# A conditioned attention layer, f32 on one core: four moves in the first two turns of a software pipeline

## The reference

```
xn = ln(x);  q = xn @ Wq + bq;  k = xn @ Wk + bk + (1 - mask) * -1e6;  v = (xn @ Wv + bv) * mask
q = softmax(q, within a head);  k = softmax(k, over the 64 tokens)
att = k^T v per head;           y = q att
scale, shift = split(silu(cond) @ W_emb + b_emb)      # one pair of 256 per batch
out = x + silu(ln2(y) * (1 + scale) + shift) @ W_out + b_out
```

## Time and profile before

| | us |
|---|---|
| median of 3 runs (lowest, highest) | 306.88 (306.3, 309.34) |
| the profiled execution: time | 307.7 |
| its span, first to last instruction | 305.8 |
| TensorE busy | 291.8 (95%) |
| VectorE busy | 272.4 (89%) |
| GpSimd busy | 244.6 (80%) |
| ScalarE busy | 237.0 (77%) |
| TensorE's granted clock, mean | 1.000 of full speed |

### The profile page before, as it was taken

The page is one execution under the profiler, slowest core; times in us unless marked ns, Lnnn a source line. Parts: engine busy times, 40 slices in busy tenths (PEclk is TensorE's granted clock), DMA queues, the critical chain, the costliest instruction groups (busy, mean ns, idle before and its releaser), DMA issues.

```text
span 305.8 us, 14375 instructions
## 1 busy us (share of the span) xinstructions
PE 291.8 (95%) x5528; PEld 248.5 (81%) x5528; DVE 272.4 (89%) x640; ACT 237.0 (77%) x592; POOL 244.6 (80%) x246
## 2 busy tenths in 40 slices
PE   7999789899999999999999999999999999989875
PEld 7578588788989888988889898889888898877655
DVE  5899999989999999999999999999999796967793
ACT  1567758787978988898979888888989798776443
POOL 2275748989998989999998989898999979873470
PEclk9999999999999999999999999999999999999999
DMA  6983430704527080815325180906251341002024
GB/s 198 315 298 109 129 115 5 236 10 117 198 66 248 1 308 1 253 56 176 133 106 203 46 263 1 298 11 231 78 169 71 90 150 53 17 4 72 4 71 137
DMA packets 28445, 38.61 MB, mean 126 GB/s; under 512 B 2433, under 2 KB 20481, under 8 KB 28418
## 3 DMA queue, kind: packets, MB, share of 16 engines
q1 hardware_dynamic: 28000, 37.94, 38.1%
q10 hardware_dynamic: 418, 0.30, 0.3%
HBM read 29.80 MB, written 8.45 MB: 125 GB/s over the span
## 4 chain that ended last, share of the span: by engine, by line
PE 82%; DVE 9%; issue 4%; POOL 2%; DMA 1%; POOLq 1%; ACT 0%; SPq 0%; DVEq 0%
PE bk L1113 27%; PE bv L1113 27%; PE by L1113 15%; PE by L1198 4%; PE by L1177 4%; PE bv L1189 4%; DVE xstat L785 2%; DMA x_all<-in_x 1%; DVE k_t L909 1%; DVE q_s L898 1%; POOLq L45 1%; DVE qmax L890 1%; DVE th L843 1%; POOL xr L485 1%; DVE ystat L986 0%
## 5 line engine op out<-in xcount | busy, mean ns | idle before, releaser
L641 ACT ACTIVATE k_t<-k_t,kmax 128x64 f32<-128x64 f32 x240 | 60.5, 336 | 6.4 <-DVE kmax L916 6.2
L476 POOL TENSOR_TENSOR x_all<-x_all,bo_all 128x1024 f32 (+1 forms) x16 | 40.1, 2508 | 0.2
L436 POOL TENSOR_TENSOR h_lo<-h_s,h_hi 128x512 fp32r<-128x512 f32 x30 | 38.3, 1297 | 0.9 <-ACT h_hi L660 0.8
L445 POOL TENSOR_TENSOR xt_raw<-xt_raw,rows 128x512 f32<-128x512 f32 x28 | 37.0, 1322 | 1.5 <-DMA rows<-rows_dram 1.5
L447 POOL TENSOR_TENSOR xt_raw<-xt_raw,rows 128x512 f32<-128x512 f32 x28 | 36.5, 1303 | 2.2
L286 POOL TENSOR_TENSOR z_s<-z_s,mod_shift 128x512 f32<-128x512 f32 x30 | 30.7, 1044 | 6.8 <-DVE z_s L930 6.8
L595 ACT ACTIVATE y_s<-y_s,yr 128x256 f32<-128x256 f32 x56 | 29.1, 593 | 3.8 <-POOL yr L468 3.8
L1113 PE MATMUL bv<-w_o_hi,h_hi 128*128 128x256 f32 x120 | 31.6, 285 | 0.0
L1113 PE MATMUL bv<-w_o_lo,h_hi 128*128 128x256 f32 x120 | 31.0, 280 | 0.0
L580 ACT ACTIVATE v_s<-bk,small 128x256 f32<-128x256 f32 x32 | 15.1, 474 | 17.7 <-PE bk L1113 16.4
L1113 PEld LDWEIGHTS by<-kv,q_t 32*64 32x64 f32 x2048 | 22.4, 130 | 6.9 <-issue 6.5
(11 more groups left out here) (163 smaller groups left out, 865.9 us busy)
## 6 DMA issues: line engine op xcount, KB each, us to landing
x_all<-in_x SPq DMA_DIRECT2D x15, 512.0 KB, 6.4
out<-x_all SPq DMA_DIRECT2D x15, 512.0 KB, 5.0
xt_raw<-in_x_t SPq DMA_DIRECT2D x14, 512.0 KB, 6.1
rows<-rows_dram SPq DMA_DIRECT2D x14, 512.0 KB, 4.2
off<-in_mask_rows SPq DMA_DIRECT2D x16, 256.0 KB, 6.1
rows_dram<-xr_rows SPq DMA_DIRECT2D x56, 1.0 KB
x_all<-in_x SPq DMA_DIRECT2D x2, 256.0 KB, 3.5
z_s<-in_w_emb SPq DMA_DIRECT2D x1, 512.0 KB, 7.2
```

Source lines behind the costliest of these rows:

```text
L436: nc.gpsimd.tensor_tensor(h_lo[:, c, :], h_s[:, c, :], h_hi[:, c, :].bitcast(fp32), ALU.subtract).then_inc(hlo_d, 1)
L445: nc.gpsimd.tensor_tensor(xc, xc, rows[:, parity, 0, :], ALU.mult).then_inc(xm_d, 1)
L476: nc.gpsimd.tensor_tensor(xg, xg, bo_all[:, :].unsqueeze(1).broadcast_to([P, T, D]), ALU.add).then_inc(xb_d, 1)
L641: last = nc.scalar.activation(kk, kk, ACT.Exp, scale=-1.0, bias=kmax[:, c, n:n + 1])
```

## The change

Four edits, all in turns 0 to 2:

1. W_out. ScalarE makes the high part in turn 0, halving in the same instruction (`weights_o_high`, between the first two `v_tile`). VectorE is left with one fused operation for the low part (`weights_o_low`).
2. The table is written to `bt[1]` (the fourth bank of `by`) in place of `be[1]` (the second). The wait of TensorE for the copies moves from `exp_k_transposed(1)` to the second half of `q_transposed(1)`, and ScalarE's copies from the end of turn 1 to the start of turn 2.
3. Group 1's `xhat`: tiles 2 and 3 go to GpSimd, behind `x_rstd(1)` in turn -1. GpSimd's `x_biased(0)` moves ahead of `x_rstd(2)`, and ScalarE's third `v_tile` of turn 0 ahead of its first exponential. VectorE's order in turn 0 is new: q's maximum and shift come between and ahead of parts of `x_stats(2)`, and `x_rows(2)` moves from ahead of `x_low(1)` to behind `x_stats(3)`.
4. In turn 1 `y_scaled_all(0)` stands ahead of `q_shifted(1, 1, 0)`.

```diff
 (GpSimd, turn -1)
                     x_rstd(1)
+                    pool.wait_ge(xt_d, 2)
+                    pool.wait_ge(xr_d, 8)
+                    for t in (2, 3):
+                        nc.gpsimd.tensor_scalar(xhat[:, t, :], x_all[:, 1, t * D:t * D + D], xr[:, 0, t:t + 1],
+                                                xr[:, 1, t:t + 1], ALU.mult, ALU.add).then_inc(xhat_d, 1)
                     return
...
 (GpSimd, turn 0)
                     k_shifted(0)
                     k_shifted(1)
+                    x_biased(0)
                     x_rstd(2)
...
-                if not last_turn(i):
-                    x_biased(i)
                 if first(i):
                     x_rstd(3)
+                elif not last_turn(i):
+                    x_biased(i)
...
 (ScalarE)
+            def weights_o_high():
+
+                act.wait_ge(wo_in, 16)
+                nc.scalar.activation(w_o_hi[:, :, :], w_o, ACT.Copy, scale=0.5).then_inc(wo_high, 1)
...
             def x_hat_one():
...
-                for t in range(T):
+                for t in (0, 1):
...
             def emb_copied():
...
-                    nc.scalar.activation(emb[:, j, :], be[1][:, j * BATCH:(j + 1) * BATCH], ACT.Identity,
+                    nc.scalar.activation(emb[:, j, :], bt[1][:, j * BATCH:(j + 1) * BATCH], ACT.Identity,
                                          scale=0.5, bias=b_e[:, j:j + 1]).then_inc(emb_out, 1)
...
+                if isinstance(i, int) and i == 2:
+                    emb_copied()
                 if O:
                     y_hat_all(i - 2)
...
                     v_tile(0, 0, 0)
+                    weights_o_high()
                     v_tile(0, 0, 1)
                     x_hat_one()
+                    v_tile(0, 0, 2)
                     k_exp_first(0)
-                    v_tile(0, 0, 2)
                     v_tile(0, 0, 3)
...
                 q_exp(i, par, 0)
-                if second(i):
-                    emb_copied()
...
 (VectorE)
-            def weights_o():
-
-                dve.wait_ge(wo_in, 16)
-                link(nc.vector.tensor_scalar(w_o, w_o, 0.5, None, ALU.mult))
-                split(w_o, w_o_hi, w_o_lo)
+            def weights_o_low():
+
+                dve.wait_ge(wo_high, 1)
+                nc.vector.scalar_tensor_tensor(w_o_lo[:, :, :], w_o, 0.5, w_o_hi[:, :, :].bitcast(fp32),
+                                               ALU.mult, ALU.subtract).then_inc(weights_ready, 1)
...
                 if first(i):
-                    x_stats(2, 0)
-                elif not (isinstance(i, int) and i + 2 >= G):
+                    q_max(0, 0)
+                    q_shifted(0, 0, 0)
+                    x_variances(2, 0, (0, 1, 2))
+                    q_max(0, 1)
+                    q_shifted(0, 0, 1)
+                    x_variances(2, 0, (3,))
+                    x_means(2)
+                    x_low(1, by[:, 2:4, :])
+                    x_stats(3, 1)
+                    x_rows(2)
+                    return
...
                 if second(i):
-                    weights_o()
+                    weights_o_low()
                     silu_cond()
...
-                if B:
-                    y_sums(i - 1)
-                q_shifted(i, par, 0)
-                if B:
+                y_sums(i - 1)
+                if second(i):
+                    y_scaled_all(0)
+                    q_shifted(1, 1, 0)
+                else:
+                    q_shifted(i, par, 0)
                     y_scaled_all(i - 1)
-                    y_stats(i - 1, (0, 1, 2, 3))
+                y_stats(i - 1, (0, 1, 2, 3))
...
 (TensorE)
-                        last = mm(be[1][:, j * BATCH:(j + 1) * BATCH], w_e[c // 2][:, c % 2, j * P:(j + 1) * P],
+                        last = mm(bt[1][:, j * BATCH:(j + 1) * BATCH], w_e[c // 2][:, c % 2, j * P:(j + 1) * P],
...
                 for e in range(2):
-                    if second(g) and e == 1:
-                        pe.wait_ge(emb_out, 2 * C)
                     wait(pe, ys_d, 2 * (g - 1) + 2)
...
                 for c in range(C):
                     wait(pe, ys_d, 2 * g)
+                    if second(g) and c == 1:
+                        pe.wait_ge(emb_out, 2 * C)
```

More of the change, by code:

```diff
@@ L175, in build_layer @@
         wqv_high = sem("wqv_high")
+        wo_high = sem("wo_high")
         mod_ready = sem("mod_ready")
@@ L772, in x_stats, with x_variances @@
             def x_stats(g, parity):
+                x_variances(g, parity, (0, 1, 2, 3))
+                x_means(g)
+            def x_variances(g, parity, tiles):
                 first = isinstance(g, int)
@@ L781, in x_stats @@
                 wait(dve, xr_d, 4 * g)
-                for t in range(T):
+                for t in tiles:
                     if first and g == 0 and t == 2:
@@ L786, in x_stats, with x_means @@
                                        .rearrange("p g n -> p (g n)")).then_inc(xstat_d, 1)
+            def x_means(g):
                 for t in range(T):
@@ L1022, in body @@
                 if first(i):
-                    x_stats(2, 0)
-                elif not (isinstance(i, int) and i + 2 >= G):
+                    q_max(0, 0)
[9 more added lines that the diff above has]
+                    return
+                if not (isinstance(i, int) and i + 2 >= G):
                     x_rows(i + 2)
```

## The result

| | before | changed |
|---|---|---|
| median of 12 runs, us (lowest, highest) | 309.04 (306.3, 311.67) | 305.6 (304.97, 306.77) |
| profiled execution, us (span) | 307.7 (305.8) | 306.03 (304.2) |
| ratio of the compared runs, 95% interval | | 0.9947 (0.9922 to 0.9973) |

The kernel is faster by 0.5% (0.3 to 0.8). The ratio leaves out the most disturbed runs, all of them of the kernel before; that is why the two medians lie 3.4 us apart, more than it says. The profiled pair differs by 1.6 us, where 2.8 were forecast.

The account below looks back on a forecast made before the run. TensorE, busy 291.8 of 305.8 us, bounds the kernel; only its waits in the first two turns can be had. 1.97 + 0.8 + 0.1 = 2.87, rounded to 2.8: 306.88 - 2.8 = 304.1 us, range 302.4 to 306.2.

Parts of the forecast that it names:

- Gap 1: TensorE's wait for y's division, ahead of the table's matmuls in turn 1; forecast to close whole, 1.97 us.
- gap 2: TensorE's wait for ScalarE's copies of the modulation table out of bank 1; forecast to go, 0.8 us.
- VectorE leaves the turn 0.4 us later: Turn 0: q_max(0, 1) and x_rows(2) delay VectorE by 0.4 us; y_product(0) has 1.0 to spare, so no cost.
- just ready: x_rstd(2) on GpSimd ends at 25.9, in time for x_rows(2), moved to about 26.5 on VectorE.
- The slower rival: Chain through GpSimd's x_rstd(2) and VectorE's x_rows(2) delays k's mask and y_product(0); kernel slower above 29.9; chance 0.04.
- point of decision (27.1): Each microsecond x_rstd(2) ends after 27.1 delays k's mask, its exponentials and y_product(0) one for one.
- Late rows: Rival: x_scaled(2) at contended price or late broadcast delays y_hat 1.0 to 1.5 us; gain 1.3 to 1.8; chance 0.17.
- one of those by which the prediction would call itself wrong: Signs of failure: new TensorE wait for y_s L595, xt_hi or xt_lo in turn 2, or idle time in the loop behind.
- VectorE does what it does in the loop: Reason for pricing x_scaled(2) at 5.3 us, the page's mean, from 33 to 38.4.
- Gap 3: TensorE's 0.8 us wait for k's exponential in the first turn; forecast to shrink by 0.1 us.

Follow-up runs that it names:

- e4: Kernel before with only W_out's high part by ScalarE and the division ahead of q's shift; ratio 0.9916.
- e11: Kernel before with only W_out's high part by ScalarE and the fused low part on VectorE; ratio 0.9874.
- e9: Changed kernel with one move undone, x_rstd(2) ahead of x_biased(0) on GpSimd again; ratio 0.9933, median 305.08 us.
- e1: Changed kernel with group 3 of x given its own statistics buffers, so x_stats(3) does not wait for x_rstd(2); ratio 0.9893, median 304.16 us.
- e2: Changed kernel with turns -1 and 0 in the order of before; W_out's high part, bank and division kept; ratio 0.9872, median 303.57 us.
- e8: e2 with one xhat tile of group 1 by GpSimd and the second exponential ahead of the fourth v_tile; ratio 0.9889, median 303.85 us.
- e6: The changed kernel run again, unaltered, on a second chip; ratio 0.9966 to before, median 305.9 us.
- e13: e2 run once more on a third chip; ratio 0.9884, median 303.57 us.
- b1: Further profile of the kernel before, unaltered; 311.02 us.
- b2: Another profile of the kernel before, unaltered; 306.55 us.
- e7: Kernel before with one added wait, GpSimd's x_scaled(2) held until VectorE is through W_out and silu_cond; ratio 0.9951.
- e3: Kernel before with only the table's bank and its wait moved; ratio 0.9961.
- b4: Kernel before with one wait on VectorE, W_out's work starting only after GpSimd's first operation of x_scaled(2); ratio 1.0121.

## Why the prediction was off

- **The time, 305.6, lies in the range, in part by luck; the size of the gain does not hold.** Forecast 2.8 us, within 1%; measured 1.6 in the profiled pair and 0.5% (0.3 to 0.8) by ratio. The range stood on a median of before of 306.88, of three runs; the twelve of the comparison gave 309.04.
- **Gap 1 and gap 2: right** (e4, e11; changed profile). The division ended at 35.63 where 34.9 to 35.5 stood, since `y_product(0)` came 0.76 late; the table's turn, late as well, came at 36.73.
- **The step that failed** is "VectorE leaves the turn 0.4 us later". I had followed the wait of `x_rows(2)` for `x_rstd(2)`, "just ready", and overlooked that `x_stats(3)`, one place ahead of it, waits for the same step (`wait(dve, xr_d, 4 * g)`). `x_rstd(2)` ended at 26.08, as forecast (25.9), in part by luck: VectorE's means, which the sum didn't have, came late enough to hold it there by themselves (e9). The one who asked for it did so at 25.0 and not at 26.5. VectorE left the turn 1.6 us later, `q_copied` was at 32.28 and no longer at 30.68, and 0.87 us came back at `y_product(0)`. The slower rival had the chain, but its point of decision (27.1) was that of `x_rows(2)`. e1 shows it by removing just this wait.
- **Late rows: right chain, wrong victim.** `x_scaled(2)` ran at 1.3 an operation, as taken, from 33.89 (33.0 forecast, late by VectorE's wait). y_hat did not wait. But ending at 39.15 it lay across VectorE's two small operations at 37.9, and one of them cost 1.1 us more; `x_low(2)` and with it K's low products and `h_s` were late by 0.3 and 0.24. The wait ahead of the low products, which read `xt_lo`, is one of those by which the prediction would call itself wrong. e1, e2 and e9, where those operations met no GpSimd operation for long, have neither wait behind `y_product(0)`; e8 shows that VectorE, made late in another way, brings back the one for `h_s`. I had excluded it by "VectorE does what it does in the loop", looking only at the large operations.
- **Gap 3: 0.1 forecast, 0.04 seen** (22.63 to 22.59).
- **The baseline.** I priced gap 1 from one profile. It is 2 us in some executions of the kernel before and 3 with a clock loss of 1.6 in others, so the change is worth more than the profiled pair says in those: 0.9 us between the medians at full clock (306.5 and 305.6), 3.4 between those of all runs in the result. The spread of the runs before was there to be read; I took it for noise.

The moves of turn 0 cost, then: they took some 2 us of the gain (e2 against e6, on two chips; e8 against e6, on one; 1.7 in TensorE's timeline). W_out's high part on ScalarE is the gain that is sure (e11). The bank takes 0.8 us of waiting away in every trace that has it, but what it is worth in time is not settled: 1.2 us from e4 to e2, and 0.2 from e11 to e13 with the division's move.

## To carry to other kernels

When steps change places, list every wait of every step that now stands behind the delayed one, in queue order; the first to ask for a result decides, not the one whose name goes with it. Where VectorE and GpSimd reach for operands in SBUF within a tenth of a microsecond of each other, the order can differ from run to run (b1, b2), and a wait that fixes it may be worth as much as taking work away. Wide spread in the runs of a deterministic kernel is a finding: profile it twice before pricing a gap from it.

## What the runs showed of the hardware

- A cast, a tensor_scalar or a two-input VectorE operation with its operands in SBUF and a GpSimd operation exclude each other, also where it is tiny: 128x4 took 1.26 us beside a 1.27 us GpSimd operation, 0.16 otherwise. The cast of 128x512 took 0.43 alone (e7) and 1.41 beside GpSimd (the kernel before). Not every operation does: four `bn_stats` took 1.39 us beside `x_scaled(2)` (changed kernel, 36.13) and 1.40 elsewhere. The Trainium skill, SBUF — State Buffer, section "Who interferes with whom", says that tensor_scalar and casts in the two-port modes contend with GpSimd too, and that issue order decides who blocks; the trace agrees (the 1.26 us operation started 0.04 behind GpSimd's).
- TensorE's clock held at 1.0 behind a wait of 1.94 us (b2) and fell to half behind waits of 2.97 to 3.47 us (e3, b1, b4). The length of the wait alone doesn't decide it: in the tail every kernel waits 1.8 to 1.9 us for the last y's, and in e8's profile, whose mean clock is 0.994, the clock fell behind that one, while behind the same wait in the changed kernel it stayed at 1.0 (four transposes took 1.06 us in e8, 0.66 there). TensorE's row and the stretch of e8, then TensorE's row of the changed kernel:

```profile
287.23 1.06 PE L1358 MATMUL by<-ident,y_s 128*128 128x128 f32 x4 [1.88 <-POOL y_s L541]
```
```profile
288.00:290.00 2.00, 2.00 (x7) 1.65 (x6) 1.97 (x4) 1.73 (x3) 1.82 (x4) 0.50 0.00 0
```
```profile
290.25 0.66 PE L1361 MATMUL by<-ident,y_s 128*128 128x128 f32 x4 [1.88 <-POOL y_s L542]
```

  Some runs of kernels without a long gap had a lower mean clock too (one of twelve of e7, one of six of e13). The tail is a place where they can have lost it; that they did is not shown, since only their time and mean clock are recorded.
- TensorE's issue gap in turn 2 (0.31 to 1.01 us here) and those from 266 us on come to 1.0 to 2.9 us in sum. They differ by 0.5 to 0.8 between profiles of one kernel (changed 2.9 and 2.4; before 2.6, 2.8 and 2.0), with no cause in the profile. Differences between single spans below a microsecond say little for that reason.
